# One-hots for twelve blocks of edges at a time, in a ring of three, in a two-layer graph network with a residual norm

## The reference

```
msg = concat[x[dst], x[src], edge_attr] @ W1 + b1      # 129 -> 128, and a loop edge per node added
h   = relu(segment_sum(msg, dst))
out = relu(segment_sum(concat[h[dst], h[src], attr] @ W2 + b2, dst))   # 257 -> 64
y   = layernorm(x + log_softmax(out))
```

## Time and profile before

| | us |
|---|---|
| median of 3 runs | 209.03 (208.85 to 209.24) |
| the profiled execution | 208.97 |
| its span, first to last instruction | 207.2 |
| TensorE busy in the span | 177.4 |
| VectorE busy | 173.8 |
| ScalarE busy | 118.8 |

### The profile page before, as it was taken

How to read it: one execution, slowest core, us unless ns; L and a number is a source line. 1 busy time by engine, 2 the same in 40 slices (tenths; PEclk the granted TensorE clock), 3 DMA queues, 4 the chain that set the end, 5 groups by cost and what they waited for, 6 DMA issues and landing times.

```text
span 207.2 us, 5086 instructions
## 1 busy us (share of the span) xinstructions
PE 177.4 (86%) x2019; PEld 162.7 (79%) x2019; DVE 173.8 (84%) x495; ACT 118.8 (57%) x234; POOL 48.9 (24%) x56
## 2 busy tenths in 40 slices
PE   0515399999999999999899999999996999999950
PEld 0104299888988989889779889798996999999940
DVE  0889999999999999999999989921019999999873
ACT  2336649778997997888889989984220201111101
POOL 8388998305000692003004000000000000000000
PEclk9999999999999999999999999999999999999997
DMA  1334101000000000000000000000000010011010
GB/s 41 106 93 116 24 4 36 0 4 2 3 0 4 0 5 0 3 1 3 0 4 0 5 0 3 2 3 0 3 0 0 3 30 10 3 40 25 22 22 20
DMA packets 8886, 3.32 MB, mean 16 GB/s; under 512 B 8146, under 2 KB 8411, under 8 KB 8861
## 3 DMA queue, kind: packets, MB, share of 16 engines
q1 hardware_dynamic: 8061, 2.04, 4.8%
q0 software_dynamic: 800, 0.93, 1.9%
HBM read 2.15 MB, written 0.81 MB: 14 GB/s over the span
## 4 chain that ended last, share of the span: by engine, by line
PE 61%; DVE 29%; issue 3%; ACT 3%; DMA 2%; DVEq 0%; ACTq 0%
PE pset L1016 17%; PE acc L975 15%; PE pset L961 13%; DVE ohr L514 8%; DVE ohl L514 7%; PE acc L1016 7%; PE epb L1002 3%; PE epb L1010 2%; DMA adj<-in_dst 2%; PE epb L990 2%; DVE adj L504 2%; ACT adj L816 1%; DVE adj L463 1%; PE epb L1003 1%; PE epb L992 1%
## 5 line engine op out<-in xcount | busy, mean ns | idle before, releaser
L816 ACT ACTIVATE adj<-pset 125x1000 bf16<-125x1000 f32 (+7 forms) x100 | 81.1, 836 | 15.1 <-PE pset L961 12.0
L975 PE MATMUL acc<-x,adj 125*125 125x195 bf16 x625 | 67.8, 252 | 0.0
L961 PE MATMUL pset<-ohr,ohl 128*125 128x125 bf16 x625 | 54.4, 232 | 8.7 <-DVE ohr L514 8.1
L961 PEld LDWEIGHTS pset<-ohr,ohl 128*125 128x125 bf16 x625 | 47.7, 146 | 13.8 <-issue 6.6
L975 PEld LDWEIGHTS acc<-x,adj 125*125 125x125 bf16 x625 | 57.1, 139 | 0.3
L514 DVE TENSOR_TENSOR ohl<-iota,keys 128x1000 bf16<-128x1000 bf16 (+1 forms) x79 | 52.5, 664 | 0.7 <-ACT keys L799 0.5
L514 DVE TENSOR_TENSOR ohr<-iota,keys 128x1000 bf16<-128x1000 bf16 (+1 forms) x79 | 52.5, 664 | 0.0
L1016 PE MATMUL pset<-z,adj 125*125 125x192 bf16 x425 | 37.0, 247 | 1.8 <-DVE x L661 1.8
L1016 PEld LDWEIGHTS pset<-z,adj 125*125 125x125 bf16 x425 | 35.5, 136 | 2.4 <-DVE x L661 2.0
L903 ACT ACTIVATE x<-x 125x192 f32<-125x192 f32 (+2 forms) x6 | 2.6, 427 | 34.5 <-DVE x L670 34.5
L384 POOL CAST stats<-se 125x15 bf16<-125x15 f32 x5 | 5.4, 1071 | 54.3 <-DMA se<-se_scratch 54.3
(11 more groups left out here) (120 smaller groups left out, 169.3 us busy)
## 6 DMA issues: line engine op xcount, KB each, us to landing
x_nat<-in_x_tiles SPq DMA_DIRECT2D x1, 406.2 KB
x_nat<-in_x_tiles SPq DMA_DIRECT2D x1, 375.0 KB
out<-x SPq DMA_DIRECT2D x2, 187.5 KB
out<-x SPq DMA_DIRECT2D x3, 93.8 KB
adj<-in_dst SPq DMA_DIRECT2D x1, 208.5 KB
out<-x SPq DMA_DIRECT2D x1, 125.0 KB
adj<-in_edges,adj POOLq DMA_INDIRECT x5, 4.3
adj<-in_edge_attr,adj POOLq DMA_INDIRECT x5, 3.5
```

What stands on the lines that cost most here:

```text
L816: ins = act.activation(adj4[0:Q, g, :, i * WD:(i + n) * WD].rearrange("p h (w e) -> p h w e", e=WD), rows[:, w - k * SET:w - k * SET + n, ...
L961: ins = pe.matmul(pset[k % 2][0:Q, i // 4, i % 4 * 128:i % 4 * 128 + WD * G], ohl[k % 3][:, i // 2, :, i % 2], ohr[k % 3][:, i // 2, :, i ...
L975: ins = pe.matmul(acc[g % 2][0:Q, 0:XW], adj4[0:Q, g, h, :], x3[:, h, :], start=(h == 0), stop=(h == G - 1))
```

## The change

One-hots are made in **chunks**: the first 8 blocks, then 12 at a time (8 to 20, 20 to 32, ..., 608 to 620), and the last 5: 53 chunks in place of 79 sets. A buffer holds 12 blocks, and the ring keeps three, now in one tensor. A chunk waits for the set that holds the last block of the chunk three before it. `build(k)` still makes 8 blocks and waits for the chunk that holds the last of them. The side steps of set k are issued after the first chunk that reaches into set k. To make room, `base` lies over `x_nat`, and x is loaded a second time into the one-hots' memory, after the last build, for the end. At the start the third one-hots come after the second `rest_of_x`, and the fourth after `low_of_x`.

```diff
+CHUNK = 12
+RING = 3
+CHUNKS = ((0, 8),) + tuple((a, min(a + CHUNK, WINDOWS)) for a in range(8, WINDOWS, CHUNK))
+
+def chunk_of(w):
+    return next(c for c, (a, b) in enumerate(CHUNKS) if a <= w < b)
...
-        base = sb("base", [Q, G, C], FP32)
+        base = x_nat
...
-        ohl = [sb(f"ohl{s}", [128, SET // 2, Q, 2], BF16) for s in range(3)]
-        ohr = [sb(f"ohr{s}", [128, SET // 2, G * WD, 2], BF16) for s in range(3)]
+        ONEHOT = CHUNK // 2 * Q * 2
+        oh_flat = sb("onehots", [128, 2 * RING * ONEHOT], BF16)
...
+        x_end = oh_flat[0:Q, 0:2 * G * C].bitcast(FP32).rearrange("p (g c) -> p g c", c=C)
...
-            def onehots(k):
-
-                n = -(-set_size(k) // 2)
-                if k >= 3:
-                    dve.wait_ge(built, k - 2)
+            def onehots(c):
+
+                a, b = CHUNKS[c]
+                n = (b - a + 1) // 2
+                if c >= RING:
+                    dve.wait_ge(built, (CHUNKS[c - RING][1] - 1) // SET + 1)
...
             onehots(0)
             onehots(1)
             bias_rest(0)
             low_of_x(0, 0, XA)
-            onehots(2)
             rest_of_x(1, XA, G)
             bias_rest(1)
+            onehots(2)
             attr_sums(0, 0, WD)
-            onehots(3)
             low_of_x(1, XA, G)
...
+            done_sets = 0
+            for c in range(3, len(CHUNKS)):
+                for j in range(1, J):
+                    if CHUNKS[c][0] <= j * Q < CHUNKS[c][1]:
+                        dve.wait_ge(keys_ready, j + 1)
+                onehots(c)
+                sets = range(done_sets, (CHUNKS[c][1] - 1) // SET + 1)
+                done_sets = sets.stop
+                for k in sets:
+                    beside(k)
...
                 if i == 0:
+                    dve.wait_ge(xend_in, 16)
                     dve.memset(f_p[:, :, C:C + 1], 0.0)
...
-                flink(dve.tensor_tensor(p, o, x_nat[:, a:b, :], ALU.add))
+                flink(dve.tensor_tensor(p, o, x_end[:, a:b, :], ALU.add))
...
-                pe.wait_ge(oh_ready, k + 1)
+                pe.wait_ge(oh_ready, chunk_of(k * SET + set_size(k) - 1) + 1)
...
+            sp.wait_ge(built, NSETS)
+            sp.dma_start(x_end, x_tiles).then_inc(xend_in, 16)
             for i, (a, b) in enumerate(BATCHES):
                 sp.wait_ge(fch, at["stored", i])
```

More of the change, by code:

```diff
@@ L162, in gnn, with onehot @@
         keyl, keyr = keys[:, 0, :], keys[:, 1, :]
-        ohl = [sb(f"ohl{s}", [128, SET // 2, Q, 2], BF16) for s in range(3)]
-        ohr = [sb(f"ohr{s}", [128, SET // 2, G * WD, 2], BF16) for s in range(3)]
+        ONEHOT = CHUNK // 2 * Q * 2
+        oh_flat = sb("onehots", [128, 2 * RING * ONEHOT], BF16)
+        def onehot(i):
+            return oh_flat[:, i * ONEHOT:(i + 1) * ONEHOT].rearrange("p (w q t) -> p w q t", q=Q, t=2)
+        ohl = [onehot(s) for s in range(RING)]
+        ohr = [onehot(RING + s) for s in range(RING)]
+        assert 2 * G * C <= RING * ONEHOT
+        x_end = oh_flat[0:Q, 0:2 * G * C].bitcast(FP32).rearrange("p (g c) -> p g c", c=C)
         x3_flat = sb("x3", [Q, G * XW + 1], BF16)
@@ L173, in gnn @@
         turn = sb("turn", [128, EP * Q], FP32)
-        turn_last = ohl[1][:, :, :, :].rearrange("p a b c -> p (a b c)").bitcast(FP32)
+        turn_last = oh_flat[:, RING * ONEHOT:RING * ONEHOT + 2 * Q].bitcast(FP32)
         def flat(i):
@@ L276, in gnn @@
         se_in = [sem(f"se_in{j}") for j in range(J)]
+        xend_in = sem("xend_in")
         o_out = [sem("o_out0"), sem("o_out1")]
@@ L506, in attr_sums @@
                                              accum_out=se_w[:, j, r:r + 1]).then_inc(se_ready, 1)
-            def onehots(k):
-                n = -(-set_size(k) // 2)
-                if k >= 3:
-                    dve.wait_ge(built, k - 2)
+            def onehots(c):
[3 more added lines that the diff above has]
+                    dve.wait_ge(built, (CHUNKS[c - RING][1] - 1) // SET + 1)
                 for oh, key in ((ohl, keyl), (ohr, keyr)):
                     ins = dve.tensor_tensor(
-                        out=oh[k % 3][:, 0:n, :, :],
+                        out=oh[c % RING][:, 0:n, :, :],
                         in0=iota2[:, 0:Q, :].unsqueeze(1).broadcast_to([128, n, Q, 2]),
-                        in1=key[:, k * SET:k * SET + 2 * n].rearrange("p (q o k) -> p q o k", o=1, k=2)
+                        in1=key[:, a:a + 2 * n].rearrange("p (q o k) -> p q o k", o=1, k=2)
                         .broadcast_to([128, n, Q, 2]),
@@ L561, in z_low, with beside @@
                    .then_inc(z3_ready, 1)
[L563 to L572, removed]
-            onehots(2)
-            rest_of_x(1, XA, G)
-            bias_rest(1)
-            attr_sums(0, 0, WD)
-            onehots(3)
[L578 to L584, removed]
+            def beside(k):
                 if k == 10:
@@ L611, in _ @@
                         z_low(i)
+            key_distances(0)
+            key_tiles(0)
+            key_sums(0)
+            rest_of_x(0, 0, XA)
+            dve.wait_ge(consts, 8)
+            dve.wait_ge(keys_ready, 1)
+            onehots(0)
+            onehots(1)
+            bias_rest(0)
+            low_of_x(0, 0, XA)
+            rest_of_x(1, XA, G)
+            bias_rest(1)
+            onehots(2)
+            attr_sums(0, 0, WD)
+            low_of_x(1, XA, G)
+            done_sets = 0
[8 more added lines that the diff above has]
+                    beside(k)
             last = len(EPILOGUES) - 1
@@ L746, in _ @@
                             dve.tensor_tensor(g_u[:, C:2 * C].unsqueeze(1), g_sum[:, bass.ds(g, 1), 0:C],
-                                              x_nat[:, bass.ds(g, 1), :], ALU.add)
+                                              x_end[:, bass.ds(g, 1), :], ALU.add)
                             dve.wait_ge(g_sems["u_ready"], 2 * g + 1)
-                            dve.tensor_scalar(g_u[:, 0:C].unsqueeze(1), x_nat[:, bass.ds(g, 1), :], g_v[:, 0:1], None, ALU.mult)\
+                            dve.tensor_scalar(g_u[:, 0:C].unsqueeze(1), x_end[:, bass.ds(g, 1), :], g_v[:, 0:1], None, ALU.mult)\
                                .then_inc(g_sems["u_ready"], 1)
@@ L764, in _ @@
                 link(dve.tensor_tensor(go[:, :, :], go[:, :, :], bc(gw), ALU.subtract))
-                link(dve.tensor_tensor(go[:, :, :], go[:, :, :], x_nat[:, :, :], ALU.add))
+                link(dve.tensor_tensor(go[:, :, :], go[:, :, :], x_end[:, :, :], ALU.add))
                 link(dve.tensor_reduce(gm[:, :], go[:, :, :], AX.X, ALU.add))
@@ L958, in build @@
                     pe.wait_ge(evac, k - 1)
-                pe.wait_ge(oh_ready, k + 1)
+                pe.wait_ge(oh_ready, chunk_of(k * SET + set_size(k) - 1) + 1)
                 for i in range(set_size(k)):
+                    w = k * SET + i
+                    c = chunk_of(w)
+                    q, t = divmod(w - CHUNKS[c][0], 2)
                     ins = pe.matmul(pset[k % 2][0:Q, i // 4, i % 4 * 128:i % 4 * 128 + WD * G],
-                                    ohl[k % 3][:, i // 2, :, i % 2], ohr[k % 3][:, i // 2, :, i % 2], start=True, stop=True)
+                                    ohl[c % RING][:, q, :, t], ohr[c % RING][:, q, :, t], start=True, stop=True)
                 ins.then_inc(built, 1)
```

## The result

The changed kernel took 217.32 us (median, 217.07 to 217.69) against 209.03 us. The ratio is 1.0398, with a 95% interval of 1.0377 to 1.0418. The forecast was 214.8 us in a range of 211.2 to 217.0: the right sign, but only two thirds of the size, and the median lies 0.3 us above the range. The profiled execution took 217.54 us with a span of 215.7.

A forecast was written before the change was run, and what follows sets the result against it. VectorE and TensorE were taken to decide in turns until the last build. Delays of 1.0 + 1.1 + 0.4 + 0.3 + 3.0 = 5.8 us on 208.97 gave 214.8 us, range 211.2 to 217.0.

The forecast's parts named there:

- The price of a chunk: VectorE's one-hots: an instruction of 1500 elements costs 0.85 us, a chunk 1.70 us.
- The fourth rival: Rival, 8%: 0.07 us more in some 30 deciding chunks, +2.1, 216.9 us; late x, up to 3 us more.
- The start: From start to set 17: longer chunks and a VectorE wait for ScalarE's cast make set 17 1.0 us later.
- the 0.1 us for `reduce_sums(0)`: Between start and set 17: VectorE loses 0.1 us at this reduction because it finds a later TensorE.
- Sets 17 to 54: Delay at builds grows from +1.0 us at set 17 to +2.1 at 26, +2.7 at 44, +2.8 after 54.
- Now 3 chunks 5.10 + 2.43 + 0.21: VectorE from `reduce_sums` at 79.26 to set 44: chunks, side steps and set 44's own, 7.74 us against 7.15.
- The late sets: Sets 57 to 78: held reductions leave VectorE a whole chunk to write before TensorE can build, +3.0 us together.
- not by the ring: When VectorE runs ahead, the next `reduce_sums` in its queue catches it, not a lack of free one-hot buffers.
- The saving: Rival, 7% with anything faster: VectorE's work decides everywhere, so 3.6 us go, 205.4 us.
- the second rival: Rival, 22%: VectorE reaches late reductions after TensorE finished the group, nothing lost there; 211.8 us, variants up to 213.
- x was not late: The second load of x, issued after the last build, is covered by 22 us; above that up to 3 us.
- nothing cancelled: Rival, 5%: gains and losses cancel within 0.2%.

The follow-up runs named there:

- all moves made: Changed kernel with side steps after the completing chunk, the old start, and `reduce_sums` and `z_rest` one set later: 208.46 us, 0.9977 of the kernel before.
- the same two moves: Kernel before, sets of 8, with `reduce_sums` and `z_rest` each one set later: 207.86 us, 0.9949.
- the kernel before with one and with two moves: Kernel before with `reduce_sums` one set later, 208.17 us, 0.9952; with `z_rest` one set later as well, 207.86 us, 0.9949.

## Why the prediction was wrong in size

**The price of a chunk: right.** A chunk of 1500 elements lasts 931 ns and two start 0.85 us apart, 1.70 for the pair (52.45 to 54.15 in VectorE's timeline). The fourth rival's dearer chunks are out.

```profile
52.45 1.78 DVE L534 TENSOR_TENSOR onehots<-iota,keys 128x1500 bf16<-128x1500 bf16 x2
54.15 0.28 DVE L504 TENSOR_SCALAR adj<-adj,thr 125x128 f32<-125x128 int32 x1
```

**The start: right in kind, short by 0.4 us.** VectorE's wait for the cast was 0.47 us (0.55 forecast). The term that was too small is the 0.1 us for `reduce_sums(0)`, which waited 0.48 us. TensorE's fast pace had come later by more than its start: build 4 was 0.9 us late, build 7 1.4 us (31.51 before, 32.87 after). Part of this can be chance, as the last section shows. The run with the old start got 0.8 us back.

**Sets 17 to 54: the step that failed.** "Now 3 chunks 5.10 + 2.43 + 0.21" for the way to set 44 took the side steps at their durations of before. I had asked of each `reduce_sums` whether VectorE would now come too early for TensorE, but not of `z_rest`, which was moved just as far and waits for ScalarE. It waited 0.80 and 0.81 us, 1.6 of the missing 2.9 us. The stretch from the reduction at 81.87 to the end of set 44's one-hots, 7.74 us in my sum, took 8.7 us, and from set 44 to set 53 it was 15.8 us where I had 14.9. Moving `z_rest` alone gave 1.9 us, 1.5 of them before build 57 and 0.3 at build 59. The `reduce_sums` at set 49 waited 1.10 us, 0.9 was forecast. The other 1.3 us are the start's 0.4, the late sets' 0.2, and some 0.7 in small pieces between sets 26 and 57, none above 0.25 us; no run separates those.

**The late sets: right.** 3.2 us against 3.0. How much later than in the kernel before the builds start shows what cost there (us, from TensorE's timelines of the profiled executions):

| kernel | build 57 | last build | grows by |
|---|---|---|---|
| changed | 5.48 | 8.68 | 3.2 |
| `z_rest` one set later | 3.94 | 6.87 | 2.9 |
| `reduce_sums` one set later | 3.68 | 4.48 | 0.8 |
| side steps after the chunk | 2.76 | 2.81 | 0.1 |
| shifted by one set | 7.58 | 8.40 | 0.8 |
| shifted by two sets | 8.41 | 8.86 | 0.5 |

All have chunks of 12 that complete sets late. With the reductions moved, most of the loss is gone though the chunks are the same, so the late completion alone isn't what costs there. In the shifted kernels the late reductions before the last build still hold VectorE, for 4.1 and 5.2 us (8.5 in the changed kernel), and most of the loss is gone too, since no half-made set waits behind them any more. It takes both, the held reduction and the half-made set.

**The ring: right for three, misread as a general rule.** I wrote that VectorE is caught "not by the ring". That holds in the kernel before and with three buffers of 12; with two it is caught by the ring and loses 8 us more.

**The rivals.** The saving doesn't carry: that rival's condition was that no reduction holds VectorE, and its price 3.6 us. With all moves made, none does until 108 us, and chunks of 12 come to 208.46 us, while sets of 8 with the same two moves come to 207.86. So even then 52 fewer instructions gain nothing. VectorE doesn't decide everywhere then either: it waits 2.9 us for free buffers, 1.9 of them before 80 us. The Trainium skill, page "Perfetto Trace Analysis", section "Optimizing Scalar/DVE Operations", says that larger operations can improve throughput if the engine is saturated, and that for an engine which isn't, but makes others wait, breaking up instructions may let work be completed sooner. By its busy time VectorE is close to the first case, with 112.5 of the 117.0 us from 20 to 137 us in the kernel before. The runs go the way of the second all the same: the chunks that hurt stand behind a wait, and TensorE waits for them. The late sets absorbing it, the second rival, is out: VectorE waited 2.38 us at the first of them. x was not late, and nothing cancelled.

## What to carry to other kernels

Where two engines take turns in deciding, ask of every step that waits, in the order of its queue, what is half done behind it, and do so for all steps that a change moves, not only for the kind that waited before. In this kernel a larger instruction saved its fixed part only where its engine decided, and cost its whole length where its engine was held just before with the consumer's unit half made; so end it where the consumer's unit ends. What a wait costs depends on its place: moving the reductions by one set gained 0.5% in the kernel before, where the larger instructions gained nothing.

## What the runs showed of the hardware

The granted clock didn't show the slow start. In both kernels it stands at 1.00, the level of 2.4 GHz, in each stretch from 16 to 34 us, but eight matmuls of a build last 1.06 to 1.09 us until 31 or 32 us and 0.65 us after. In the changed kernel these rows of TensorE's timeline show the step:

```profile
31.05 1.06 PE L992 MATMUL pset<-onehots 128*125 128x125 bf16 x8
...
32.87 0.65 PE L992 MATMUL pset<-onehots 128*125 128x125 bf16 x8
```

The engine had worked without a gap since build 4, at 26.70 us in this kernel and at 25.76 us in the one before, where the step lies between 30.11 and 31.51 us. No run was made to tell what sets its time, and it isn't fixed by what the kernel did: in four executions in which build 4 starts at 25.76 or 25.77 us (the kernel before, the run with chunks of eight, and the kernel before with one and with two moves), build 7 starts at 31.51, 31.22, 31.97 and 31.32 us. Between the last two 0.35 us of that is still there at set 17.

The time of a VectorE instruction on one-hots is a straight line in its elements: 281 ns for 250 and 669 for 1000, 931 for 1500 in the changed kernel and 1189 for 2000 in the run with chunks of 16, which is 0.52 ns an element in each step. The distances agree: 0.85 us for 1500 elements and 0.59 for 1000.
